# A recurrent two-layer kernel on one core: one more bias addition on GpSimd in four batches, and the routing scatters spread differently

## What is computed

```python
# attention of layer 0: 16 heads of 8 features, a relative bias clipped at 128
scores = einsum('bhqd,bhkd->bhqk', Q, K) / sqrt(8) + rel_bias_matrix[None]
out = einsum('bhqk,bhkd->bhqd', softmax(scores), V) ... @ Wo.T + bo
# ffn of layer 0: 8 experts, top 2 of a softmax gate, plus 0.5 * gelu(x @ shared_W + shared_b)
```

## Time and profile before

| | us |
|---|---|
| runs | 794.53, 797.87, 796.08 |
| median | 796.08 |
| span of the profiled execution | 796.5 |
| TensorE busy | 690.3 (87%) |
| VectorE busy | 553.2 (69%) |
| ScalarE busy | 490.2 (62%) |
| GpSimd busy | 450.4 (57%) |

### The profile page before, as it was taken

How to read it: one execution, slowest core, us unless ns; L and a number is a source line. 1 busy time by engine, 2 the same in 40 slices (tenths; PEclk the granted TensorE clock), 3 DMA queues, 4 the chain that set the end, 5 groups by cost and what they waited for, 6 DMA issues and landing times. The chain is left out here.

```text
span 796.5 us, 17035 instructions
## 1 busy us (share of the span) xinstructions
PE 690.3 (87%) x5313; PEld 472.2 (59%) x5313; DVE 553.2 (69%) x1291; ACT 490.2 (62%) x934; POOL 450.4 (57%) x397
## 2 busy tenths in 40 slices
PE   3886888999999999879999889899897688999890
PEld 2651222333333333349998778789887577998790
DVE  6999999998998888743433367836828995543346
ACT  4763687788788888864554536578682365544351
POOL 5942445899999999773554544410005776554342
PEclk9998999999999999989999999999999899999995
DMA  7984541233222223137886896660001523787875
GB/s 222 276 236 133 165 132 55 75 78 100 86 86 86 79 88 98 45 98 234 244 265 214 247 297 194 189 184 1 2 1 34 170 62 97 223 237 221 252 226 165
DMA packets 96461, 117.44 MB, mean 147 GB/s; under 512 B 10552, under 2 KB 72296, under 8 KB 96408
## 3 DMA queue, kind: packets, MB, share of 16 engines
q1 hardware_dynamic: 88376, 100.22, 43.1%
q0 software_dynamic: 8032, 16.58, 5.9%
HBM read 82.30 MB, written 34.32 MB: 146 GB/s over the span
## 5 line engine op out<-in xcount | busy, mean ns | idle before, releaser
L756 POOL DMA_INDIRECT yg_dram<-work x135 | 133.0, 985 | 146.8 <-DVE work L1946 107.8
L1351 ACT ACTIVATE work<-wide,work 128x256 f32<-128x256 f32 (+1 forms) x324 | 130.7, 468 | 131.4 <-PE wide L976 130.2
L1509 DVE TENSOR_REDUCE work<-wide 128x4 bf16<-128x1024 f32 x128 | 155.7, 1226 | 20.2 <-PE wide L853 19.3
L987 PE MATMUL wide<-work 128*128 128x128 f32 x1272 | 155.1, 275 | 0.0
L987 PEld LDWEIGHTS wide<-work 128*128 128x128 f32 x1272 | 149.4, 192 | 0.8
L976 PE MATMUL wide<-xT,work 128*128 128x256 f32 (+1 forms) x552 | 131.5, 382 | 11.8 <-issue 7.0
L976 PEld LDWEIGHTS wide<-xT,work 128*128 128x128 f32 x552 | 98.7, 191 | 26.9 <-issue 13.9
L717 POOL TENSOR_TENSOR work<-work,biasT 128x1024 f32<-128x1024 f32 x32 | 75.8, 2370 | 43.0 <-ACT work L1289 42.5
L717 POOL TENSOR_TENSOR yy<-yy,biasT 128x1024 f32<-128x1024 f32 x32 | 75.8, 2368 | 24.0 <-ACT yy L1289 23.5
L1296 ACT ACTIVATE yy<-yy 128x1024 f32<-128x1024 f32 x64 | 67.4, 1054 | 26.4 <-DVE yy L1817 23.8
L847 PE MATMUL wide<-biasA,turnb 128*128 128x512 bf16 x256 | 79.3, 392 | 3.3 <-DVE work L1509 3.0
(11 more groups left out here) (318 smaller groups left out, 1210.8 us busy)
## 6 DMA issues: line engine op xcount, KB each, us to landing
work<-in_wcat SPq DMA_DIRECT2D x73, 578.0 KB, 4.4
xg_dram<-empty SPq DMA_DIRECT2D x35, 260.0 KB, 2.8
work<-xg_dram SPq DMA_DIRECT2D x66, 130.0 KB
stk_dram<-yy SPq DMA_DIRECT2D x16, 384.0 KB, 3.6
work<-stk_dram SPq DMA_DIRECT2D x64, 96.0 KB
work<-stk_dram SPq DMA_DIRECT2D x64, 64.0 KB
yy<-yg_dram SPq DMA_DIRECT2D x8, 512.0 KB, 6.7
biasT<-ext_dram SPq DMA_DIRECT2D x8, 384.0 KB, 5.5
```

The costliest lines, as they stand in the source:

```text
L756: g.indirect_dma_start(out=yg_dram[l], out_offset=bass.IndirectOffsetOnAxis(ap=yid[v][:, s_:s_ + 1].bitcast(u32), axis=0), in_=yb[u][:, s_ ...
L987: last = mm(YP[u][:, s_ * D:(s_ + 1) * D], hb[u][:, c, s_ * P:(s_ + 1) * P], wb[v][:, HID + c * D:HID + (c + 1) * D], start=(c == 0), stop ...
L1351: A(hb[u][:, c, 0:n * P], bank[2 + 2 * u + c // 2][:, (c % 2) * TS:(c % 2) * TS + n * P], ACT.Gelu, bias=wb[v][:, bc:bc + 1]).then_inc(m[" ...
L1509: V.tensor_reduce(nmax[:, :, 2 * place(t):2 * place(t) + 2].rearrange("p c e -> p e c"), into[:, :].rearrange("p (e c k) -> p e c k", e=2, ...
```

## The change

GpSimd adds the bias of five pairs (0, 2, 3, 4, 6) in batches 0 to 3 and of four (0, 2, 4, 6) afterwards; pair 3 leaves VectorE in these four batches, where its scores are copied out by ScalarE like those of the even pairs. The counts of the semaphores follow from `moved` and `added`. ScalarE takes the scores of pair 3 between the exponentials of pair 0 and the copy of the values, and its exponentials come behind the copy of the next batch's first maxima. VectorE's routing pieces stay at t = 1, 3, 5, 7; the one of t = 3 has no addition ahead of it in these batches. GpSimd scatters from batch 3's pair 0 on, once behind each pair that it adds and twice behind pair 6: six times in batch 3 and five times in each later batch, until the 64 are out. Batches 2 and 3 are written out on TensorE and ScalarE.

```diff
+FIVE = 4
+
+def by_pool(b):
+    return (0, 2, 3, 4, 6) if isinstance(b, int) and b < FIVE else (0, 2, 4, 6)
+
+def moved(b, t):
+    if isinstance(b, int) and b < FIVE:
+        return b * 5 + sum(p < t for p in by_pool(b))
+    return b * 4 + (FIVE + sum(p < t for p in by_pool(FIVE)))
+
+def added(b, t):
+    if isinstance(b, int) and b < FIVE:
+        return b * 3 + sum(p not in by_pool(b) for p in range(t))
+    return b * 4 + (sum(p not in by_pool(FIVE) for p in range(t)) - FIVE)
...
             def add_bias_pool(b, t):
-                pool.wait_ge(A0["Sa"], b * (NPAIR // 2) + (t // 2 + 1))
+                pool.wait_ge(A0["Sa"], moved(b, t) + 1)
...
                 for b in range(NB):
-                    for t in range(0, NPAIR, 2):
+                    for t in by_pool(b):
                         add_bias_pool(b, t)
-                        if b == 3 and t == 4:
+                        if b == 3 and t == 0:
                             pool.wait_ge(s_xgz[0], NEMPTY[0] * 16)
                             pool.wait_ge(pre[0]["T"], NB)
-                        for _ in range(2 if t in (2, 6) else 1):
-                            if (b >= 4 or b == 3 and t >= 4) and sent < TOPK * T:
+                        for _ in range(2 if t == 6 else 1):
+                            if b >= 3 and sent < TOPK * T:
...
             def exp_scores(b, u, t):
-                if t % 2:
-                    pe.wait_ge(a["Sa"], b * (NPAIR // 2) + (t // 2 + 1))
+                if t and t - 1 in by_pool(b):
+                    pe.wait_ge(a["Sa"], moved(b, t))
                 elif not isinstance(b, int) or b or t:
-                    pe.wait_ge(a["Sv"], b * (NPAIR // 2) + t // 2)
+                    pe.wait_ge(a["Sv"], added(b, t))
...
             def exponentials(b, t):
-                if t % 2:
-                    act.wait_ge(a["Sv"], b * (NPAIR // 2) + (t // 2 + 1))
+                if t in by_pool(b):
+                    act.wait_ge(a["Sp"], moved(b, t) + 1)
                 else:
-                    act.wait_ge(a["Sp"], b * (NPAIR // 2) + (t // 2 + 1))
+                    act.wait_ge(a["Sv"], added(b, t) + 1)
...
                 exponentials(b, 0)
+                five = 3 in by_pool(b)
+                if five:
+                    take_scores(b, 3)
                 if ahead:
                     fetch_values(b + 1, 1 - u)
-                exponentials(b, 3)
+                if not five:
+                    exponentials(b, 3)
                 take_scores(b, 4)
                 exponentials(b, 2)
                 if ahead:
                     copy_maxima(b + 1, 0)
+                if five:
+                    exponentials(b, 3)
                 exponentials(b, 5)
...
             def attend_dve(b, back=2, ahead=True, part=None):
                 for t in range(NPAIR):
-                    if t % 2:
+                    if t not in by_pool(b):
                         add_bias(b, t)
-                        if part is not None:
-                            route_first_layer(part, t)
+                    if t % 2 and part is not None:
+                        route_first_layer(part, t)
```

More of the change, by code:

```diff
@@ L965, in _ @@
             attend(1, 1, 1, back=1)
-            with pe.Fori(0, NB // 2 - 2) as it:
-                attend(it * 2 + 2, 0, it + 1)
-                attend(it * 2 + 3, 1, it + 2)
+            attend(2, 0, 1)
+            attend(3, 1, 2)
+            with pe.Fori(0, NB // 2 - 3) as it:
+                attend(it * 2 + 4, 0, it + 2)
+                attend(it * 2 + 5, 1, it + 3)
             attend(NB - 2, 0, NB // 2 - 1)
@@ L1332, in _ @@
             attend_act(1, 1, back=1)
-            with act.Fori(0, NB // 2 - 2) as it:
-                attend_act(it * 2 + 2, 0)
-                attend_act(it * 2 + 3, 1)
+            attend_act(2, 0)
+            attend_act(3, 1)
+            with act.Fori(0, NB // 2 - 3) as it:
+                attend_act(it * 2 + 4, 0)
+                attend_act(it * 2 + 5, 1)
             attend_act(NB - 2, 0)
```

## The result

The changed kernel takes 817.48 us (median of 812.15, 815.29, 819.67 and 821.51) against 796.85 of the kernel before (four runs, 794.53 to 797.87): ratio 1.0246, 95% interval 1.0194 to 1.0297 (here and below the ratio is not exactly the quotient of the two medians). It is slower, as forecast, but by 20.6 us where the sum said 7.8, and lies outside the range.

What follows compares the result with a forecast made beforehand. VectorE was taken to set the pace in batches 1 to 3 of the first attention, GpSimd from batch 6. The sum was 796.08 - 3.25 + 6.2 + 4.9 = 803.9 us, range 796.5 to 808.0.

Steps and rivals of the forecast that it cites:

- Part 1: Batches 4 to 13: five scatters a batch instead of six let batches run at 16.48 us; gain 3.25 us.
- rival (d): Batches 4 to 13: GpSimd stays pace-maker despite five scatters, no gain, 807.2 us; chance 0.12 together with worse holds.
- Part 3: Hand-over to the experts: three scatters left for batch 15 delay the tiles' rows; 4.9 us lost, bounds 3.3 and 6.
- Rival (b): Batches 0 to 3 and hand-over: no holds occur and the hand-over is hidden too, 791.6 us; chance 0.08.
- Part 2: Batches 0 to 3: pair 3's move to GpSimd makes its additions hold VectorE's routing operations; 6.2 us lost.
- rival (a): Batches 0 to 3: VectorE's operations slip in before GpSimd's next addition, no holds, 1.2 us gained, 796.5 us; chance 0.20.
- the sum of 0.3, 1.9, 2.0 and 2.0: Losses forecast for batches 0, 1, 2 and 3 from VectorE operations held by GpSimd additions; 6.2 us in all.
- my outer bound of 4.0: Batch 1: loss in us if both L1638 and L1639 are held; 1.9 was taken, for L1638 alone.
- 20.2 us of work in 19.1: Batch 3: GpSimd's six scatters (7.6), five additions (11.9) and a marking (0.7) against a batch of 19.1 us.
- Rival (c): Batches 1 to 3: both batch 1 operations wait, later ones lose whole additions, 806.0 us; chance 0.12 together with rival (d).

Runs made afterwards that it cites:

- e10: Kernel before with four GpSimd pairs throughout, six scatters in batches 3, 6, 9 and 12, five in other later batches, none left for batch 15; ratio 0.9981.
- e8: Changed kernel with five GpSimd pairs in batches 0 to 2 only, four in batch 3; ratio 1.0161 to the kernel before.
- e12: Changed kernel with 38, 26 and 34 unread matmuls in TensorE's long waits of batches 1, 2 and 3; 844.46 us beside 831.21 for the kernel before.
- e1: Changed kernel with the old spread of scatters, from pair 4 of batch 3 and six a batch; ratio 1.015 to the kernel before.
- e2: Changed kernel's scatters, six in batch 3 from pair 0 on, with four GpSimd pairs in every batch; ratio 1.0009 to the kernel before.
- e6: Changed kernel with VectorE's routing pieces of pairs 3 and 5 in batches 1 to 3 moved to where GpSimd rests; ratio 1.0073 to the kernel before.
- e5: The changed kernel itself run again, unaltered, beside other runs on the same chip; ratio 1.0169 to the kernel before.

## Why the prediction was right in direction and wrong in size

**Part 1, right.** Batches 4 to 12 took 16.48 and batches 4 to 13 gained 3.35; 3.25 was forecast. GpSimd has gaps (0.42 to 0.61 ahead of three of its additions between 209 and 226), and rival (d) falls. e10 adds that a sixth scatter in every third batch also fits.

**Part 3, right, with some luck in the size.** 4.2 measured, 4.9 forecast, bounds 3.3 to 6. The chain came as laid out: the last scatter behind pair 4, the rows of tile 0 2.35 behind its start, TensorE idle 2.71 ahead of tile 1, where I had 3. The rows of tile 1 needed 3.7 from their issue at 359.77, as the 3.6 of the earlier trace rows said. What I did not have is that TensorE's clock fell to 0.50 at 351, 20 us behind batch 14's mark where it had been 27 before, and that TensorE came to the transposes of tile 0 1.3 us later by itself (29.10 behind the mark, before 27.84). Rival (b) falls. Run e8, whose last scatter stands one pair later, lost another 4.4.

**Part 2, right in kind and mis-sized: 15.2 against 6.2.** The holds occur; rival (a) falls. The step that failed is the sum of 0.3, 1.9, 2.0 and 2.0, for three reasons.
- *The count of holds* (in the line numbers of the kernel before, 32 lower than in the rows above). I took one hold in batch 1 (L1638) and one in batch 3 (L1707). In a chain in which each operation waits for the last, each starts just behind the end of an addition, and where GpSimd's additions stand back to back it meets the next. Batch 1: both L1638 and L1639, my outer bound of 4.0, and more, since they cost 4.1 by themselves and L1636 another 0.55. Batch 3: L1702, L1707 and L1709, 5.7 together instead of one hold. L1702 I had even counted as evidence for rival (a), and L1523 too, wrongly (see the last section). Batch 2 was laid out as it came: L1663 and L1664 held to 126.70, and here the forecast of 2.0 was the nearest (2.0 by the holds, 2.9 with the clock). Batch 0: L1588 held for 1.6.
- *The clock.* I charged half clock only at the hand-over. A hold stops TensorE for 3 to 5 us, and behind each such wait it ran at 0.50 for some microseconds. By the growth of the period less the growth that holds explain (held time less 1.13 for the addition saved) this is 1.8, 0.9 and 1.0 us in batches 1 to 3 and 1.5 in batch 0; e12 measured 1.8 to 2.2, 0.8 and 1.3 in the three (1.1 and 1.6 against e1 in the first two). No run fills the waits of batch 0, so that its 1.5 is the clock's is not shown; its clock fell from 0.83 to 0.70.
- *The scatters.* I priced them as load (20.2 us of work in 19.1). They act by place: as spacers they move the additions onto later routing pieces. e1 has five additions without these scatters and e2 and e8 have four additions with them, at no loss in batch 3; together they lost 5.7 in the one profile and 1.9 in the other.

Held time less the addition saved is 0.7 + 3.6 + 2.0 + 4.8 = 11.1, the rest 5.2, less the 1.1 by which batch 0's mark came early: 15.2. Rival (c), worse holds, was the one that came true, and its price of 806.0 was itself too low, as it knew nothing of L1702, L1709 and the clock. A bound should have been the whole chain times a whole addition, as I had it for batch 1 and not for batches 2 and 3: the seven operations that were held come to some 15 us at 2.1 each. That they are seven is known only now.

## What to carry to other kernels

Before work is moved to GpSimd, list VectorE's small operations between SBUF tiles that run meanwhile: a chain of them loses up to one whole GpSimd instruction per link, so count links, not pieces, and bound by all of them, or by GpSimd's instructions in that time if they are fewer. Reductions, memsets and operations with PSUM operands are safe beside it, so a remedy is to order VectorE's stream with GpSimd as loaded as it is (e6: 5.9 and 3.6 us back in batches 1 and 2; in batch 3, where the new places met additions again, none). A wait of several microseconds that a hold puts on TensorE must be priced with the half clock behind it, and work that is spread later for one engine's sake must still end before the first reader of its last piece.

## What the hardware showed that I had not expected

- Two instructions of VectorE and GpSimd that want the same way into SBUF and start 0.33 us apart can go either way, L1741 with 0.20 or 2.75 us, which makes one kernel's batch 21.1 or 24.9 us long.
- A held operation does its own work after the addition: L1670 with 16 columns ends 0.03 us behind it (102.29 and 102.26), L1739 with 320 columns 0.35 (153.29, the addition 150.56 plus 2.38).
- Filling half of a 4.6 us wait of TensorE with matmuls (2.36 of it) left the clock to fall to 0.50; filling 4.32 of it kept it at 1.00.
- Not every GpSimd instruction holds VectorE. In the kernel before, VectorE's L1523, a sum of two SBUF operands, kept its 0.68 when it started inside GpSimd's tensor_scalar L665 (22.68, inside the one of 21.75 to 23.00), and it was GpSimd's that got longer: L665 took 0.79 from 12.6 to 16.5, while VectorE did statistics, and mostly 1.05 to 1.40 beside L1523 and its neighbours. So this was no evidence that a sum slips past an addition, as I used it for rival (a), and the hold of GpSimd by VectorE, which I said no row showed, was in that trace. Why this pair goes the other way is open.
- GpSimd's scatters don't hold VectorE as its additions do: in e5 L1741, a sum of two SBUF operands, ran its usual 0.20 from 154.79 inside the scatter of 154.04 to 155.09.
